# Attention outputs of two heads accumulated in the same PSUM rows, denominators by products with ones, in an eight-stage transformer kernel

## What is computed

```python
q = (x @ wq + bq).reshape(B, N, 16, 16).transpose(0, 2, 1, 3)
k = (ctx @ wk + bk).reshape(B, N, 16, 16).transpose(0, 2, 1, 3)
v = (ctx @ wv + bv).reshape(B, N, 16, 16).transpose(0, 2, 1, 3)
scores = jnp.einsum('bhqd,bhkd->bhqk', q, k) / jnp.sqrt(16)
scores = jnp.where(mask, -jnp.inf, scores)
attn = jax.nn.softmax(scores, axis=-1)
out = jnp.einsum('bhqk,bhkd->bhqd', attn, v).transpose(0, 2, 1, 3).reshape(B, N, 256)
x = layernorm(x + out @ wo + bo)
```

## Time and profile before

| | |
|---|---|
| Median of 3 runs | 1161.72 us (1161.29 to 1163.68) |
| The profiled execution | 1159.94 us, its span 1157.7 us |
| PE busy | 1106.9 us (96%), 13908 matmul records |
| PEld busy | 921.1 us (80%) |
| DVE busy | 841.3 us (73%) |
| ACT busy | 618.6 us (53%) |
| POOL busy | 258.8 us (22%) |
| Granted clock of PE, mean | 0.99 |

### The profile page before, as it was taken

One profiled execution on the slowest core, in us unless ns is written; L12 is line 12 of the kernel. 1 busy time (PEld: TensorE's weight loads), 2 busy tenths in 40 slices (PEclk: granted clock), 3 DMA queues, 4 the chain that ended last, 5 costly groups with the idle time before them and its releaser, 6 DMA issues. The chain is left out here.

```text
span 1157.7 us, 36414 instructions
## 1 busy us (share of the span) xinstructions
PE 1106.9 (96%) x13908; PEld 921.1 (80%) x13908; DVE 841.3 (73%) x3468; ACT 618.6 (53%) x1584; POOL 258.8 (22%) x383
## 2 busy tenths in 40 slices
PE   6999999999999999999999999999999999999886
PEld 5878778888778788878888887888888878787665
DVE  4466987957878687697687777786778685987841
ACT  3644455455555556545556565655556455545453
POOL 0322412203121230222304032320321223121100
PEclk9999999999999999999999999999999999999997
DMA  9600010200111001010010202001010100110000
GB/s 339 246 11 2 2 48 11 84 20 2 28 40 28 39 16 52 2 41 26 16 52 2 66 2 66 2 16 52 16 52 2 52 2 2 52 47 7 2 6 10
DMA packets 21224, 45.11 MB, mean 39 GB/s; under 512 B 2496, under 2 KB 14912, under 8 KB 18112
## 3 DMA queue, kind: packets, MB, share of 16 engines
q1 hardware_dynamic: 19952, 41.36, 10.1%
q10 hardware_dynamic: 1104, 1.44, 0.4%
HBM read 40.70 MB, written 2.10 MB: 37 GB/s over the span
## 5 line engine op out<-in xcount | busy, mean ns | idle before, releaser
L663 POOL TENSOR_TENSOR root<-var_eps,halves 128x1 f32<-128x1 f32 x128 | 76.9, 602 | 609.9 <-DVE var_eps L1171 588.1
L971 ACT ACTIVATE exps_t<-bank 128x512 f32<-128x512 f32 x256 | 135.7, 605 | 34.3 <-PE bank L795 33.8
L1111 DVE CUSTOM_DVE_ANT_0 bank<-bank,bias 128x128 f32<-128x128 f32 x512 | 130.1, 324 | 18.8 <-PE bank L763 18.8
L721 PE MATMUL bank<-x_t,weights_A 128*128 128x128 f32 x1024 | 139.3, 284 | 2.7 <-ACT x_t L931 2.1
L721 PEld LDWEIGHTS bank<-x_t,weights_A 128*128 128x128 f32 x1024 | 127.3, 197 | 12.1 <-ACT x_t L931 4.5
L721 PE MATMUL bank<-x_t,weights_F 128*128 128x128 f32 x1024 | 127.9, 281 | 2.8 <-ACT x_t L931 1.7
L721 PEld LDWEIGHTS bank<-x_t,weights_F 128*128 128x128 f32 x1024 | 121.6, 195 | 9.1 <-ACT x_t L931 3.1
L808 PE MATMUL bank<-exps_t,v_one 128*32 128x128 f32 x3072 | 114.5, 277 | 8.2 <-DVE exps_t L1083 6.1
L714 PE MATMUL bank<-weights_F,exps_t 128*128 128x256 f32 x512 | 121.1, 383 | 0.2 <-DVE neg_max L1111 0.2
L763 PE MATMUL bank<-k_eo,q_t 32*128 32x256 f32 x1536 | 107.7, 396 | 2.6 <-issue 1.7
L1111 DVE DVE_READ_ACCUMULATOR2_ANT neg_max<- 128x1 f32 x768 | 106.5, 139 | 0.1
(11 more groups left out here) (112 smaller groups left out, 1964.8 us busy)
## 6 DMA issues: line engine op xcount, KB each, us to landing
weight<-in_fside SPq DMA_DIRECT2D x16, 1024.0 KB, 4.9
weights_A<-in_weights_A SPq DMA_DIRECT2D x4, 1028.0 KB, 15.3
weights_F<-in_weights_F SPq DMA_DIRECT2D x2, 2054.0 KB, 17.9
drop_raw<-in_drop SPq DMA_DIRECT2D x16, 256.0 KB, 5.3
x_hat<-in_x SPq DMA_DIRECT2D x16, 128.0 KB, 2.5
out<-x_sum SPq DMA_DIRECT2D x16, 128.0 KB, 1.7
ctx_t<-in_ctx_t SPq DMA_DIRECT2D x13, 128.0 KB, 3.0
rows_A<-in_rows_A SPq DMA_DIRECT2D x3, 512.0 KB, 15.4
```

Of the source, the lines that this page charges most:

```text
L663: nc.gpsimd.tensor_tensor(root[x][:], var_eps[x][:], halves[:, e:e + 1], ALU.pow).then_inc(done["root"], 1)
L721: mm = nc.tensor.matmul(dst[:, 128 * f:128 * f + 128], w[:, c, 128 * f:128 * f + 128], tokens_t[:, c, :], start=(c == 0), stop=(c == KC - 1))
L971: nc.scalar.activation(dst, score_bank(x, "ST", s, j)[:], ACT.Exp, scale=DH ** -0.5).then_inc(done["exp"], 1)
L1111: ins = nc.vector.tensor_tensor_reduce(out=heads[:, n, :], in0=heads[:, n, :], in1=mask_bias(x, s), scale=-1.0, scalar=2.0 ** 126, op0=ALU ...
```

## The change

- `outputs` is now two steps, one for each half of the groups. In a half, 8 matmuls with values write the columns of one of two chunks, and 8 matmuls with ones the columns of another chunk, which is 16 matmuls; there were 16 in a whole pass. The stationary operand has 32 columns for a pair of heads: for the even head its values beside 16 zeros, for the odd head 16 zeros beside its values. The two matmuls of a pair accumulate on the same 32 rows (start with the even head, stop with the odd one). `v_pairs` holds values, zeros, values for each of 8 pairs, and `ones_pair` ones, zeros, ones.
- So each output stands on a row, queries on columns, and its denominator in the same row and column of another chunk of the bank. DVE takes the reciprocal of all 2 x 128 denominators a partition (L1120 of the changed file, into the buffer of x_t) and multiplies (L1122) straight into `o_t`, which PE multiplies by w_o. The steps o_raw, oT, nT and o_t are gone, and `o_raw` with `OUT_PLACES`.
- The first half's products wait for the second group of exponentials (or their masks), the second half's for the fourth.
- x is loaded in the order in which PE first uses it (elements 2, 1, 3, 4, 5, 0), by turns on SP's and ACT's queues, ahead of the key masks and of the second half of the A0 weights.
- All order tables are new.

```diff
-EXP_BUFFERS, OUT_BUFFERS, PAIR_BUFFERS = 3, 2, 3
-VE = DH + 1
+EXP_BUFFERS, PAIR_BUFFERS = 3, 3
+
+VP = 3 * DH
+HALVES = 2
...
-        yield from (("PV", s, j) for j in range(GROUPS))
+        yield from (("PV", s, half) for half in range(HALVES))
         if ATTN[s]["feeds"]:
             yield "V", ATTN[s]["feeds"]
-        yield from (("oT", s), ("nT", s), ("O", s))
+        yield "O", s
...
 TENSOR = """
-12345112112332124001001124551111001122210200010202203000120100001023032323103000230330303010011011201124101000001221
+21345112112322314001002114551102201120000120024300100010220413110131100010020120323013010000102101022222331000021300
...
-        v_one = per_set("v_one", [128, H * VE + 2 * DH - VE])
+        v_pairs = per_set("v_pairs", [128, H // 2, 3, DH])
+        ones_pair = sb("ones_pair", [128, 3, DH])
...
-        o_raw = [sb(f"o_raw{b}", [128, GROUPS, N]) for b in range(OUT_BUFFERS)]
-        recip = per_set("recip", [128, H])
-        o_t = q_t
+
+        o_t, recip = q_t, x_t
...
-                load_x(sp, 0)
+                for x in FIRST[::2]:
+                    load_x(sp, x)
                 load_keys(sp)
-                for x in range(1, SETS):
-                    load_x(sp, x)
                 load_stage(sp, "A1")
...
-                def outputs(x, s, j):
+                def of_pair(values, odd):
+
+
+                    return values[:, odd:odd + 2, :].rearrange("p a d -> p (a d)")
+
+                def outputs(x, s, half):
                     made = "later" if s == "A0" else "keep" if s in ("A2", "A5") else "exp"
-                    pe.wait_ge(done[made], nth(x, made, s, j))
-                    if j == 0:
+                    groups = (2 * half, 2 * half + 1)
+                    pe.wait_ge(done[made], nth(x, made, s, groups[-1]))
+                    if half == 0:
                         pe.wait_ge(values_made(s), nth(x, "v", s))
-                        pe.wait_ge(buffers_cleared, 3 * SETS)
+                        pe.wait_ge(buffers_cleared, 2 * SETS + 2)
                         free_bank((x, "PV", s, 0))
-                    for n in range(GH):
-                        mm = nc.tensor.matmul(bank((x, "PV", s, 0))[32 * n:32 * n + 32, 128 * j:128 * j + 128], v_one[x][:, VE * head(j, n):VE * head(j, n) + 2 * DH],
-                                              exps_t[EXP_AT[x, s]][:, GH * j + n, :], start=True, stop=True)
+
+                    for chunk in (half, KC + half):
+                        for odd in range(2):
+                            for at, (j, c) in enumerate((j, c) for j in groups for c in range(KC)):
+                                values = v_pairs[x][:, GROUPS * c + j] if chunk < KC else ones_pair
+                                mm = nc.tensor.matmul(bank((x, "PV", s, 0))[32 * at:32 * at + 32, 128 * chunk:128 * chunk + 128],
+                                                      of_pair(values, odd), exps_t[EXP_AT[x, s]][:, GH * j + 2 * c + odd, :],
+                                                      start=(odd == 0), stop=(odd == 1), skip_group_check=True)
                     mm.then_inc(done["PV"], 1)
...
                 act.dma_start(weights["A0"][:, 0:half], dram["weights_A0"][:, 0:half]).then_inc(first_loaded, 16)
+                for x in FIRST[1::2]:
+                    load_x(act, x)
                 act.dma_start(weights["A0"][:, half:], dram["weights_A0"][:, half:]).then_inc(stage_loaded["A0"], 16)
...
-                    dve.wait_ge(done["oT"], nth(x, "oT", s))
-                    heads = bank((x, "oT", s))[:].rearrange("p (h e) -> p h e", h=H)
-                    nc.vector.reciprocal(recip[x][:].unsqueeze(2), heads[:, :, DH:DH + 1]).then_inc(recip_made, 1)
+                    dve.wait_ge(done["PV"], nth(x, "PV", s, HALVES - 1))
+                    chunks = bank((x, "PV", s, 0))[:].rearrange("p (c q) -> p c q", c=2 * KC)
+                    nc.vector.reciprocal(recip[x][:], chunks[:, KC:, :]).then_inc(recip_made, 1)
                     dve.wait_ge(recip_made, nth(x, "o_norm", s))
-                    nc.vector.tensor_tensor(o_norm[x].rearrange("p (h d) -> p h d", h=H), heads[:, :, 0:DH],
-                                            recip[x][:].unsqueeze(2).broadcast_to([128, H, DH]), ALU.mult
-                                            ).then_inc(done["o_norm"], 1)
+                    nc.vector.tensor_tensor(o_t[x][:], chunks[:, 0:KC, :], recip[x][:], ALU.mult).then_inc(done["o_norm"], 1)
```

More of the change, by code:

```diff
@@ L214 @@
[L214 to L218, removed]
@@ L302 @@
         NTH[_beat] = _seen[_beat[1]] = _seen.get(_beat[1], 0) + 1
-TAKEN_BY = {"fold": "folded", "xT": "x_t", "K": "k_eo", "Q": "q_t", "V": "v", "mT": "m_t", "oT": "o_norm", "nT": "o_t", "O": "sum",
-            "Y": "sum", "H": "h_t"}
+TAKEN_BY = {"fold": "folded", "xT": "x_t", "K": "k_eo", "Q": "q_t", "V": "v", "mT": "m_t", "O": "sum", "Y": "sum",
+            "H": "h_t"}
 SCORES = ("S", "ST")
@@ L330 @@
 EXP_AT, EXP_BEFORE = shared_places(EXP_PLACES, [b for b in SCALAR_ORDER if b[1] in ("exp", "h_t") and b[3] == 0])
-OUT_AT, OUT_BEFORE = shared_places(OUT_PLACES, [b for b in SCALAR_ORDER if b[1] == "o_raw"])
+FIRST = [beat[0] for beat in TENSOR_ORDER if beat[1:] == ("xT", "A0") and beat[0] < SETS]
 WEIGHT_TURNS = [beat[0] for beat in SYNC_ORDER if beat[1] == "load_weight"]
@@ L396, in program @@
         x_t = per_set("x_t", [128, KC, N])
-        o_norm = [t[:].rearrange("p c q -> p (c q)") for t in x_t]
         ctx_t = per_set("ctx_t", [128, KC, N])
@@ L452, in program @@
         stored = sems("stored")
-        done = {k: sem(f"done_{k}") for k in ("xT", "K", "Q", "S", "V", "mT", "ST", "shift", "PV", "oT", "nT", "O",
+        done = {k: sem(f"done_{k}") for k in ("xT", "K", "Q", "S", "V", "mT", "ST", "shift", "PV", "O",
                                               "H", "Y", "fold")}
-        done |= {k: sem(f"done_{k}") for k in ("x_t", "square", "v_copy", "k_copy", "q_t", "m_t", "exp", "o_raw", "o_t", "h_t")}
+        done |= {k: sem(f"done_{k}") for k in ("x_t", "square", "v_copy", "k_copy", "q_t", "m_t", "exp", "h_t")}
         done |= {k: sem(f"done_{k}") for k in ("bias", "pairs", "folded", "k_eo", "v", "times", "lower", "max", "high_low", "keep", "o_norm", "sum",
@@ L510, in taken @@
             elif kind == "PV":
-                taker = ("o_raw", s)
+                taker = ("o_norm", s)
             elif kind == "V":
@@ L525, in slots @@
             return slice(GH * j, GH * j + GH)
-        def heads_of(values):
-            return values[:, 0:H * VE].rearrange("p (h e) -> p h e", h=H)
         def hidden(x, s):
@@ L583, in _ @@
             def _(sp):
-                load_x(sp, 0)
+                for x in FIRST[::2]:
+                    load_x(sp, x)
                 load_keys(sp)
-                for x in range(1, SETS):
-                    load_x(sp, x)
                 load_stage(sp, "A1")
-                for x in range(3, SETS):
+                for x in FIRST[::2]:
                     load_ctx(sp, x)
@@ L913, in free_values @@
                 if before := stage_before(x, s):
-                    engine.wait_ge(done["PV"], nth(before[0], "PV", before[1], GROUPS - 1))
+                    engine.wait_ge(done["PV"], nth(before[0], "PV", before[1], HALVES - 1))
                 engine.wait_ge(done["V"], nth(x, "V", s))
-                return (heads_of(v_one[x])[:, :, 0:DH], bank((x, "V", s))[:, 0:D].rearrange("p (h d) -> p h d", h=H))
+                return (v_pairs[x][:, :, 0:3:2, :], bank((x, "V", s))[:, 0:D].rearrange("p (g a d) -> p g a d", a=2, d=DH))
             @block.scalar
@@ L922, in _ @@
                 act.dma_start(weights["A0"][:, 0:half], dram["weights_A0"][:, 0:half]).then_inc(first_loaded, 16)
+                for x in FIRST[1::2]:
+                    load_x(act, x)
                 act.dma_start(weights["A0"][:, half:], dram["weights_A0"][:, half:]).then_inc(stage_loaded["A0"], 16)
-                for x in range(3):
+                for x in FIRST[1::2]:
                     load_ctx(act, x)
```

137 lines of the change are left out of this document (58 added, 79 removed).

## The result

The changed kernel takes **1279.39 us** (median of 3 runs, 1278.55 to 1281.36). Against the kernel before the ratio is 1.1011, 95% interval 1.0984 to 1.1039: 118 us slower. The forecast was 1176 us with a range of 1152 to 1200, so the direction was right and the size was not.

A forecast was written before the change was run, and what follows sets the result against it. PE was taken to set the time, DVE second. 1159.9 us profiled + 8 (PE) + 10.5 (handoff) - 3 (head) - 0.6 (tail) = 1174.8, with 1.8 for the median 1176 us; range 1152 to 1200.

The forecast's parts named there:

- PE's pace: PE's matmuls: 0.22 us a round; output products +78 us, transposes -65, idle before them -5, together +8 us.
- the upper bound of 23 us: PE's output products: worst case, each of 384 new accumulating rounds waits for the one before; taken as 0.
- ACT: ACT: the copies o_raw and o_t go, nothing is moved onto it; its lower load is worth nothing by itself.
- The reciprocal: DVE, denominators: 256 elements per partition, where 16 were before, take 1.64 us; the other bound was 0.42 or 0.5 us.
- Rivals A and B: A: cheap reciprocal, shorter chain pays, 1156 us, chance 0.27; B: cheap or around 1 us, idle stays, 1164 us, chance 0.20.
- Rival D: DVE's reciprocal at eight cycles an element: 2.13 us, chain 2.8 us, 21 handoffs short, 1187 us; chance 0.05.
- DVE's busy time: DVE over all 96 passes: 133 us more, 975 us in all, 83% of the new time.
- The handoff: From last output product to product with w_o: chain 2.3 us, 19 of 96 handoffs have less, +10.5 us.
- The sign that I had named for this: PE's idle growing before scores and shifts, released by maxima, rather than before w_o, would show the forecast wrong; no size.
- Rival C: DVE's lateness reaches PE everywhere, before other elements' maxima and maskings: a quarter of 133 us, 1199 us; chance 0.20.
- Head: Start of the kernel: x issued earlier, so the first projection starts about 3 us earlier, -3 us (0 to 4.5).
- Tail: End of the kernel: last chain falls from 3.6 to 2.3 us, four rounds after the last masking add 0.65: -0.6 us.

The follow-up runs named there:

- e6: Changed kernel with the long reciprocal replaced by a copy of 16 elements and the outputs multiplied by ones: 1174.55 us, ratio 1.0112.
- e1: Changed kernel with the 256-element reciprocal replaced by a copy of the same shape: 1178.31 us, ratio 1.0146.
- e2: Changed kernel with the reciprocal replaced by a copy, and an unread 256-element reciprocal of constants added behind the multiplication: 1285.97 us, ratio 1.1084.
- e3: Kernel before, own order, with an unread 256-element reciprocal of constants added behind DVE's multiplication in each pass: 1270.97 us, ratio 1.0943.
- e5: Kernel before with 176 unread reciprocals of 128 constants put where its trace shows DVE idle: 1166.97 us, ratio 1.0042.
- e10: Changed kernel with all four engines' tables re-ordered by a replay using the measured 1.75 us reciprocal, nothing added or removed: 1214.58 us, ratio 1.0466.
- e4: Kernel before with only the new loading of x: order of first use, two queues by turns, ahead of key loads: 1158.44 us, ratio 0.9973.

## Why the prediction was right and wrong

- **PE's pace: right.** 0.22 us a round, no wait for the accumulation; the upper bound of 23 us was not needed, and PE's busy time without the long reciprocal is 3.9 to 7.6 us above that of the kernel before (e6, e1), where the sum had +8. That the whole of the change without its DVE work costs 13 us (e6), and not 4, lies in the wait for the second and fourth groups, +12 us by the rows, a term that the sum lacked.
- **ACT: not contradicted.** Its 81 us less show no gain; it waits 166.6 us for neg_mean where it waited 84.5. No run took this term apart.
- **The reciprocal: right,** 1.75 us against 1.64. Rivals A and B fall with it. Rival D, eight cycles an element, falls too: the trace has 6.25 ns an element from 128 to 256. The Trainium skill (VectorE: DVE Perf Modes, in the section on the fixed hardware budget) states a repeat count of 8 for the reciprocal, not a time; eight cycles at the 0.96 GHz of its Specifications would be 8.33 ns, an estimate that is above the trace. The recorded 2.13 us also leaves out the start that its 289 ns for 16 elements contains; with it the reading gives 2.29 us.
- **DVE's busy time: right,** 985 us against 975. The 83% of the new time became 77%, since the time grew.
- **The handoff: the step that failed.** "What they are short of adds up to 10.5 us. PE runs its list in order, so everything behind the product with w_o waits too." I laid a chain of 2.3 us along PE's list and took DVE to be free when each chain began. It wasn't in 68 of 96 passes, and the waits for q_t were 62.7 us. So the sum gave 10.5 us to the 133 us of added DVE work, all of it at this handoff, and put what comes late elsewhere behind the reciprocal in DVE's list at nothing. Measured, the long reciprocal costs 101 us (e1). e2 shows that even a sound count of the chain would have missed: with the chain short and the load behind it the time is 1286. The sign that I had named for this, idle of PE in front of scores and shifts released by maxima, did not show: PE's waits for neg_max are 3.9 us (3.8 before). In this kernel the lateness shows at the multiplication itself; in e2, where the load stands behind it, PE waits 22.7 us for neg_max.
- **Rival C named the mechanism and had the size wrong.** I gave it a quarter of DVE's added time, because a stretch with DVE at 53.84 of 60 us had cost PE nearly nothing. What reached the end was 0.80 of it (e1 to the changed kernel: 101 of 126 us) and 0.74 in e3 (109 of 148 us of busy time). "It decides where DVE is above some nine tenths for whole stretches" was wrong as well: at 78% of the span it decides. A busy stretch shows that DVE's work costs PE little where it stands in that order; it says nothing of work put in at other places. e5 at 86% and e3 at 78% are the two sides of that.
- **The new tables.** The sum took them as they are. The note under rival A, that places of 1.3 us fit a chain of 1.15 us, was a hint that they may suit a short reciprocal. e10 shows that they leave at least 65 us that an order with the measured reciprocal gets back. For what lengths they were made no run shows.
- **Head: right in kind, a little more,** 3.85 us against 3 at the first projection (2.8 in e4, where it is kept to the end). **Tail:** the last chain is 2.6 us where it was 3.6, and the drain is as long as before; too small to be seen apart.

By runs the 118 us are: 13 from the outputs, their waits, head and tail together (e6); 4 more with a copy of 256 elements in place of 16 (e1), which is within the spread of e6; 101 from the reciprocal's length. Of the 118 us at least 65 are a matter of order (e10): by the listed waits some 42 of them were waits for q_t and 17 were waits for masked exponentials. How much more of the 118 us a better order would win back stays open.

## What to carry to other kernels

In a kernel with fixed in-order lists, price time that is added on an engine that isn't the bottleneck by what stands behind it, not by the engine's share: here 0.7 to 0.8 us a microsecond at 73% busy (0.66 for the first 63 us, 0.95 for the next), and 0.03 in the engine's idle places. A cheap test is a dummy instruction of the same length in the kernel before: e3 alone shows a loss of 109 us where the long reciprocal costs 101 in the changed kernel. That the two are so near is partly luck, since their orders differ. Where the price is high, re-plan all the lists with the measured length, or split the edit and keep the part that pays for itself (e4). Here re-planning alone was not enough: e10 is still 4.7% slower than the kernel before.

## What was unexpected of the hardware

A float32 reciprocal on DVE costs 164 ns for 1 element a partition, 251 for 16, 951 for 128, 1751 for 256 from PSUM, and 1742 from SBUF: 6.25 ns for each further element from 16 on, some 4 times a copy's (227 ns for 128, 419 ns for 256), and the source hardly matters. And where PE stalled more, its busy time was longer too, by 30 us for the same 13908 records in e3, but not in e5 (1107.6 us), which has the added work without the stalls. Part of that goes with the granted clock, 0.977 in e3 and 0.991 in e5.
